# The loop over pairs of token tiles of a Mamba and MLP layer, written out

## The chip, the cores and the metric

The kernel runs on one core of a Trainium2 chip. The metric is the device time of one execution in microseconds. Engines are named as in the profile: PE (TensorE matmul), PEld (its weight loads), DVE (VectorE), ACT (ScalarE), POOL (GpSimd), SP (SyncE, which here only issues transfers). A q behind a name (DVEq) is the engine's queue, in which register and branch instructions run.

## What is computed

The input is x of 4 x 1024 tokens with 256 features. Cut to what matters:

```
x = x + attn(layernorm(x))
x = x + ffn(layernorm(x))
attn(u):  z, x, B, C, dt = split(rmsnorm(u) @ in_proj.T);  dt = softplus(dt @ dt_proj.T + dt_b)
          h = exp(dt * A) * h + (dt * x) * B      # step by step along the tokens
          y = sum over the state of h * C         # 8 groups, 32 states, 32 channels each
          h = u + ((y + x * D) * silu(z)) @ out_proj.T
          h + (silu(n @ gate.T) * (n @ up.T)) @ down.T,  n = rmsnorm(h)
ffn(x):   hidden = silu(x @ W1.T) * (x @ W3.T);  fwht(hidden) @ W2.T
```

## The kernel before, in words

The 4096 tokens are worked through in 8 tiles of 512, two tiles for each of the 4 sequences. An even tile starts a sequence; an odd one goes on with the state that the even one left in `carry`.

For one tile there are 64 units (U). A unit is one scan over 512 tokens for 128 rows of state. The chain of a unit: PE spreads a row of dt into a bank `p_dt` (`spread`, L413; three banks), ACT takes the exponential in it (`decay`, L551), DVE scans (`scan`, L791) with `bt_s`, the driven input. For each pair of units DVE (L776) or POOL (L968) first multiplies `bt_s` with B, and POOL afterwards multiplies `h_s` with C (L988; in even tiles the last column is kept in `carry` before, L985). PE adds up the states of four units in `p_y` (`sum_states`, L424).

The dense work of neighbouring tiles is laid between the units. `body(i, par, pre, units, post)` is one turn of 64 slots u: it holds the units of tile i (`units`), the projections for tile i + 1 (`pre`), and the end of tile i - 1, that is out projection, MLP and second block (`post`). Which dense step stands in which slot comes from the table STEPS, made once by `place_steps`. Every engine has its own `body`, and `bodies` calls it in the same order on each of the five: written out for -1, 0 and 1, then a loop of two passes over the pairs (2, 3) and (4, 5), then written out for 6, 7 and 8. par is i modulo 2 and picks buffers; it is a constant, so a loop body holds two turns.

At a turn's start, on DVE: the last work of the turn before (L868, the low part of dt; L905, the last addition to `res`), the product L776, scans u = 0 to 3, then L798 and L804, which finish y of tile i - 1 and wait for PE's last sum of its states (L424).

All engines meet over semaphores that only count up. So a wait for tile i is a wait for a count such as i * U + u + 1. In a body that is written out i is a Python integer and the count a constant. In the loop i is a register value, and the count is worked out by a register operation on the engine's queue ahead of the wait. `known(i)` tells the two apart; `from_tile(i, least)` is true in the loop, where i is at least 2.

In DVE's scan (L780 to L792) the waits stand in this order: a_dA (the exponential), for even u the driven input (g_bt or v_bt) and, in odd tiles, the carry (g_car), then pe_y. PE's spread waits for the scan that last used the bank.

Of the kernel before, what the change touches and what calls it, by code (L numbers as in the profile page):

```python
# [26 lines left out]
LAST = TILES - 1  # L27
# [87 lines left out]
def build(nc, x, in_w, dt_w, dt_b, a_log, d_par, out_w, gu_w, down_w, n1, n2, w1, w3, w2, ident, pick, ysel, had, out):  # L115
    with ExitStack() as ctx:
# [110 lines left out]
        def bodies(eng, body):  # L227


            body(-1, 1, True, False, False)  # L230
            body(0, 0, True, True, False)
            body(1, 1, True, True, True)
            with eng.Fori(1, LAST // 2) as pair:
                body(pair * 2, 0, True, True, True)
                body(pair * 2 + 1, 1, True, True, True)
            body(LAST - 1, 0, True, True, True)
            body(LAST, 1, False, True, True)
            body(LAST + 1, 0, False, False, True)
# [13 lines left out]
        def _(sp):  # L252
# [66 lines left out]
            def body(i, par, pre, units, post):  # L319
# [11 lines left out]
                for u in range(U):  # L331
# [8 lines left out]
                    if pre:  # L340
# [16 lines left out]
                        if u == 63:  # L357
                            keep_rows(nt, 1 - par, 1)
                            load_b(nt, 1)
                            load_dt(nt, 1)  # L360

            bodies(sp, body)
            sp.wait_ge(l_out, 16 * TILES)


        @block.tensor
        def _(pe):
# [144 lines left out]
            pe.wait_ge(w_in, 2)  # L512
            pe.wait_ge(l_w["c"], 80)
            bodies(pe, body)


        @block.scalar
        def _(act):
# [221 lines left out]

            x_spread(0)
            bodies(act, body)


# [345 lines left out]
```

## Time and profile before

| | us |
|---|---|
| median of 3 runs | 1263.95 (1263.41 to 1265.72) |
| the profiled execution | 1264.71 |
| its span, first to last instruction | 1263.0 |
| PE busy | 1080.1 |
| DVE busy | 1065.1 |
| POOL busy | 958.0 |
| ACT busy | 636.1 |
| mean granted clock of TensorE | 0.936 of full speed |

Busy times are sums over the whole span; the first tiles and the end are less full than the middle. Register, branch and transfer-issuing instructions are not in them. The profile says for each idle stretch of an engine which event ended it; "issue" means that the engine waited for nothing that the profile shows.

### The profile page before, as it was taken

What the parts mean: (1) busy time and instruction counts of PE and PEld (TensorE: products, weight loads), DVE (VectorE), ACT (ScalarE), POOL (GpSimd) and SP (SyncE); (2) the same over time, 40 slices, a digit from 0 to 9 for tenths busy, and PEclk for the clock granted to TensorE, in tenths of its full rate; (3) what the DMA queues carried; (4) which work ended last, traced back from release to release, by engine and by line L of the source; (5) the groups of instructions that cost most, each with busy time, mean ns of one, the idle gap of its engine ahead of it and who ended that gap; (6) DMA issues with size and microseconds to landing.
All of it is one profiled execution on the core that took longest, in us unless ns stands there. A gap on an engine that the chain in (4) does not pass through costs nothing.

```text
span 1263.0 us, 14738 instructions
## 1 busy us (share of the span) xinstructions
PE 1080.1 (86%) x3848; PEld 542.2 (43%) x3848; DVE 1065.1 (84%) x1193; ACT 636.1 (50%) x1142; POOL 958.0 (76%) x580
## 2 busy tenths in 40 slices
PE   2475649999798979899898989899898979898888
PEld 1121214535344444445444444445443544446445
DVE  3288999999998989999899889998999889996222
ACT  3755365545655465545655555545654545442210
POOL 0389998887998788887998888887998789865100
PEclk9676679999998999999899989999999999898889
DMA  5797867574866666684767675684766666650000
GB/s 195 170 250 162 200 152 164 121 179 105 196 134 155 146 156 144 133 187 112 173 136 164 141 165 130 135 187 110 188 135 142 147 154 133 134 117 17 1 0 17
DMA packets 99511, 176.55 MB, mean 140 GB/s; under 512 B 12960, under 2 KB 21600, under 8 KB 98784
## 3 DMA queue, kind: packets, MB, share of 16 engines
q1 hardware_dynamic: 98272, 171.36, 59.7%
q0 software_dynamic: 1152, 4.19, 0.9%
q8 instruction: 34, 0.56, 0.2%
q14 instruction: 53, 0.43, 0.1%
HBM read 150.34 MB, written 8.39 MB: 126 GB/s over the span
## 4 chain that ended last, share of the span: by engine, by line
POOL 29%; issue 25%; PE 16%; ACT 2%; DVE 2%; POOLq 1%; DVEq 0%; ACTq 0%
POOL h_s L988 16%; POOL bt_s L968 7%; PE p_r L458 5%; PE p_r L469 5%; PE p_r L464 2%; PE p_dt L413 2%; PE p_y L424 2%; POOL carry L985 1%; PE p_r L475 1%; POOL sp_l L999 1%; DVE h_s L791 1%; POOL res L1017 1%; POOL sp_w L1003 1%; POOL rs L957 1%; ACT p_dt L551 1%
## 5 line engine op out<-in xcount | busy, mean ns | idle before, releaser
L988 POOL TENSOR_TENSOR h_s<-h_s,c_s 128x1024 f32<-128x1024 f32 x256 | 607.9, 2376 | 104.5 <-DVE h_s L791 94.5
L551 ACT ACTIVATE p_dt<-p_dt,an_s 128x512 f32<-128x512 f32 x512 | 334.5, 658 | 308.1 <-PE p_dt L413 307.7
L413 PE MATMUL p_dt<-kdt,pick_s 128*128 128x512 f32 x512 | 349.5, 692 | 77.9 <-DVE h_s L791 75.5
L791 DVE TENSOR_TENSOR_SCAN h_s<-p_dt,carry,bt_s 128x512 f32<-128x512 f32 x256 | 320.6, 1270 | 14.1 <-ACT p_dt L551 13.6
L791 DVE TENSOR_TENSOR_SCAN h_s<-p_dt,bt_s 128x512 f32<-128x512 f32 x256 | 304.1, 1210 | 31.8 <-ACT p_dt L551 25.4
L469 PE MATMUL p_r<-nT,w_s 128*128 128x512 f32 x512 | 243.8, 604 | 5.4 <-ACT nT L716 5.4
L968 POOL TENSOR_TENSOR bt_s<-bt_s,b_s 128x1024 f32<-128x1024 f32 x96 | 227.2, 2367 | 19.1 <-DMA bt_s<-dx_rows 18.4
L413 PEld LDWEIGHTS p_dt<-kdt,pick_s 128*128 128x128 f32 x512 | 101.3, 201 | 222.9 <-DVE h_s L791 139.4
L776 DVE TENSOR_TENSOR bt_s<-bt_s,p_b 128x1024 f32<-128x1024 f32 x160 | 192.9, 1205 | 2.2 <-DMA bt_s<-dx_rows 1.0
L458 PE MATMUL p_r<-nT,gu_s 128*128 128x512 f32 x352 | 169.9, 603 | 2.3 <-ACT nT L711 2.3
L424 PE MATMUL p_y<-h_s,ysel_s 128*32 128x512 f32 x1024 | 150.5, 663 | 21.5 <-POOL h_s L988 21.5
L469 PEld LDWEIGHTS p_r<-nT,w_s 128*128 128x128 f32 x512 | 95.0, 191 | 122.4 <-issue 114.0
L475 PE MATMUL p_r<-w_s,hd_s 128*128 128x256 f32 x512 | 125.0, 385 | 0.0
L444 PE MATMUL p_r<-uT_s,in_s 128*128 128x512 f32 x192 | 107.2, 666 | 12.5 <-ACT uT_s L653 5.6
L475 PEld LDWEIGHTS p_r<-w_s,hd_s 128*128 128x128 f32 x512 | 96.7, 191 | 28.8 <-issue 14.9
L464 PE MATMUL p_r<-down_s,hd_s 128*128 128x256 f32 (+1 forms) x384 | 100.8, 394 | 0.0
L458 PEld LDWEIGHTS p_r<-nT,gu_s 128*128 128x128 f32 x352 | 64.8, 191 | 79.4 <-issue 73.6
L738 ACT ACTIVATE th_s<-p_r 128x512 f32<-128x512 f32 x64 | 38.2, 597 | 119.7 <-PE p_r L469 119.7
L464 PEld LDWEIGHTS p_r<-down_s,hd_s 128*128 128x128 f32 (+1 forms) x384 | 68.1, 188 | 35.2 <-issue 25.9
L930 DVE SCALAR_TENSOR_TENSOR th_s<-th_s,p_r 128x512 f32<-128x512 f32 x64 | 43.1, 674 | 35.6 <-ACT th_s L738 35.3
L439 PE MATMUL p_r<-ident_s,tok 128*128 128x128 f32 x192 | 31.8, 312 | 44.9 <-ACT tok L568 33.0
L985 POOL TENSOR_TENSOR carry<-h_s,one_s 128x2 f32<-128x2 f32 x128 | 30.1, 236 | 47.2 <-DVE h_s L791 46.3
(92 smaller groups left out, 857.3 us busy)
## 6 DMA issues: line engine op xcount, KB each, us to landing
bt_s<-dx_rows SPq DMA_DIRECT2D x512, 256.0 KB, 5.4
kdt<-st_dt SPq DMA_DIRECT2D x64, 128.0 KB, 3.8
tok<-in_x SPq DMA_DIRECT2D x8, 512.0 KB, 6.9
xr_s<-xb_s SPq DMA_DIRECT2D x64, 64.0 KB, 4.0
dx_rows<-sp_w SPq DMA_DIRECT2D x16, 256.0 KB, 2.0
b_s<-xb_s SPq DMA_DIRECT2D x64, 64.0 KB, 2.0
xo<-in_x SPq DMA_DIRECT2D x8, 512.0 KB, 7.1
out<-res POOLq DMA_DIRECT2D x8, 512.0 KB, 6.3
```

Source lines behind the costliest of these rows:

```text
L413: nc.tensor.matmul(p_dt[DT_BANK[u]][:, :], sel, kdt[:, h, p // 16, :], start=True, stop=True)\
L424: last = nc.tensor.matmul(p_y[32 * j:32 * j + 32, :], ysel_s[:, 28 - 4 * row:60 - 4 * row], h_s[:, u % 8, :], start=(m % 8 == 0), stop=(m ...
L444: ins = nc.tensor.matmul(ps[:, :], in_s[:, j, blk, :], uT_s[:, u_par, j, :], start=(j == 0), stop=(j == 1))
L458: ins = nc.tensor.matmul(ps[:, :], gu_s[:, j, blk, :], nT[:, j, :], start=(j == 0), stop=(j == 1))
L464: ins = nc.tensor.matmul(ps[:, D * (j // 6):D * (j // 6) + D], hd_s[0:n_in, f, P * s:P * s + P], down_s[0:n_in, f, :], start=(f == 0), sto ...
L469: ins = nc.tensor.matmul(ps[:, :], (w1_s if stage == "w1" else w3_s)[:, j, P * k:P * k + P], nT[:, j, :], start=(j == 0), stop=(j == 1))
L475: ins = nc.tensor.matmul(ps[:, D * (j // 8):D * (j // 8) + D], hd_s[:, f, P * s:P * s + P], w2_s[:, f, :], start=(f == 0), stop=(f == HB - 1))
L551: A(p_dt[DT_BANK[u]][:, :], p_dt[DT_BANK[u]][:, :], ACT.Exp, scale=an_s[:, c:c + 1]).then_inc(a_dA, 1)
L776: V.tensor_tensor(bt_s[:, two, :], bt_s[:, two, :], p_b[:, :].unsqueeze(1).broadcast_to([P, 2, T]), ALU.mult).then_inc(v_bt, 1)
L791: V.tensor_tensor_scan(h_s[:, u % 8, :], p_dt[DT_BANK[u]][:, :], bt_s[:, u % 16, :], carry[:, u:u + 1] if par else 0.0, ALU.mult, ALU.add) ...
L968: G.tensor_tensor(bt_s[:, two, :], bt_s[:, two, :], b_s[:, h, :].unsqueeze(1).broadcast_to([P, 2, T]), ALU.mult).then_inc(g_bt, 1)
L988: G.tensor_tensor(h_s[:, two, :], h_s[:, two, :], c_s[:, h, :].unsqueeze(1).broadcast_to([P, 2, T]), ALU.mult)\
```

## The change

The hardware loop becomes a Python loop. Each engine's program now holds the bodies of tiles 2, 3, 4 and 5 one behind the other, with constants as counts.

```
@@ -230,7 +230,7 @@
             body(-1, 1, True, False, False)
             body(0, 0, True, True, False)
             body(1, 1, True, True, True)
-            with eng.Fori(1, LAST // 2) as pair:
+            for pair in range(1, LAST // 2):
                 body(pair * 2, 0, True, True, True)
                 body(pair * 2 + 1, 1, True, True, True)
             body(LAST - 1, 0, True, True, True)
```

LAST is 7, so pair is 1 and 2 in both. What the engines compute and the order in which they do it stay. The register operations (in these listings ISA and REGISTER_ALU) and the branch go.

DVE at the top of the loop, before (L776 is the driven input, L791, listed as SCALAR_TENSOR_TENSOR, the scan, L798 the end of y):

```order
L233 UNCONDITIONAL_BRANCH
L233 ISA
L775 ISA
L776 TENSOR_TENSOR bt_s<-bt_s,p_b 128x1024
L781 ISA
L784 ISA
L790 ISA
L791 SCALAR_TENSOR_TENSOR h_s<-p_dt,bt_s 128x512
L781 REGISTER_ALU
```

The same place in the changed kernel:

```order
L868 TENSOR_TENSOR st_dt<-sp_l,st_dt 128x512
L905 TENSOR_TENSOR res<-p_r,res 128x512
L776 TENSOR_TENSOR bt_s<-bt_s,p_b 128x1024
L791 SCALAR_TENSOR_TENSOR h_s<-p_dt,bt_s 128x512 x2
L776 TENSOR_TENSOR bt_s<-bt_s,p_b 128x1024
L791 SCALAR_TENSOR_TENSOR h_s<-p_dt,bt_s 128x512 x2
L798 SCALAR_TENSOR_TENSOR p_y<-xr_s,par_s,p_y 128x512
```

Nothing is left between the vector instructions.

PE at the top of the loop, before (L413 is the spread, L424 the sum of states, L444 the projections from uT_s, L439 transposes):

```order
L424 MATMUL p_y<-h_s,ysel_s 32x512 x4
L413 MATMUL p_dt<-kdt,pick_s 128x512
L233 UNCONDITIONAL_BRANCH
L233 ISA
L413 MATMUL p_dt<-kdt,pick_s 128x512
L381 REGISTER_ALU
L402 ISA
L442 ISA
L444 MATMUL p_r<-uT_s,in_s 128x512
```

And in the changed kernel:

```order
L424 MATMUL p_y<-h_s,ysel_s 32x512 x4
L413 MATMUL p_dt<-kdt,pick_s 128x512 x2
L444 MATMUL p_r<-uT_s,in_s 128x512 x2
L413 MATMUL p_dt<-kdt,pick_s 128x512
L439 MATMUL p_r<-ident_s,tok 128x128 x8
```

The matmuls follow one another in the same order, without the branch.

## Rows read from the trace of the kernel before

**Rows 1.** The page, busy time by engine (share of the span)

```profile
PE 1080.1 (86%) x3848; PEld 542.2 (43%) x3848; DVE 1065.1 (84%) x1193; ACT 636.1 (50%) x1142; POOL 958.0 (76%) x580
```

**Rows 2.** Windows, tiles 1 to 6: us, busy by engine, granted clock, DMA share, GB/s

```profile
181.14:321.18 140.04, 129.35 (x484) 66.28 (x480) 133.70 (x148) 77.80 (x141) 116.59 (x57) 0.98 0.66 147
321.18:460.87 139.69, 129.59 (x488) 65.78 (x480) 128.54 (x150) 77.74 (x142) 122.02 (x88) 0.98 0.66 150
460.87:601.47 140.60, 128.77 (x484) 65.53 (x480) 134.44 (x150) 77.60 (x142) 117.72 (x58) 0.98 0.66 151
601.47:742.47 141.00, 131.40 (x479) 66.92 (x476) 128.67 (x149) 77.85 (x141) 121.94 (x88) 0.96 0.67 149
742.47:884.68 142.21, 131.81 (x491) 66.31 (x489) 134.42 (x150) 78.42 (x142) 117.66 (x58) 0.97 0.65 149
884.68:1022.98 138.30, 126.94 (x488) 64.97 (x480) 127.11 (x141) 77.51 (x138) 121.87 (x88) 1.00 0.66 148
```

**Rows 3.** Line L233: count, duration ns min/median/max, first and last start

```profile
L233 DVEq FUSED_REGOPS  x2: 63/63/63, 320.6 to 604.1; - x2
...
L233 PEldq FUSED_REGOPS  x2: 50/50/50, 321.3 to 605.6; - x2
...
L233 DVEq COMPARE_BRANCH  x2: 55/59/63, 601.1 to 884.1; - x2
...
L233 PEldq COMPARE_BRANCH  x2: 83/2012/3942, 601.6 to 884.8; - x2
```

**Rows 4.** Timeline of DVE, tile 4: start, us, line, what, [idle before, releaser]

```profile
601.39 1.35 DVE L868 TENSOR_TENSOR st_dt<-sp_l,st_dt 128x512 fp32r<-128x512 f32 x1
...
604.32 1.22 DVE L776 TENSOR_TENSOR bt_s<-bt_s,p_b 128x1024 f32<-128x1024 f32 x1 [0.98 <-issue]
...
613.13 0.76 DVE L798 SCALAR_TENSOR_TENSOR p_y<-xr_s,par_s,p_y 128x512 f32<-128x512 f32 x1 [1.94 <-PE p_y L424]
```

**Rows 5.** Timeline of PE behind the branch

```profile
605.72 0.49 PE L413 MATMUL p_dt<-kdt,pick_s 128*128 128x512 f32 x1 [1.76 <-issue]
```

**Rows 6.** Timeline of DVE, start of tile 2

```profile
321.10 1.34 DVE L868 TENSOR_TENSOR st_dt<-sp_l,st_dt 128x512 fp32r<-128x512 f32 x1
...
330.93 0.76 DVE L798 SCALAR_TENSOR_TENSOR p_y<-xr_s,par_s,p_y 128x512 f32<-128x512 f32 x1 [1.15 <-PE p_y L424]
```

**Rows 7.** Timeline of DVE, start of tile 6

```profile
884.60 1.34 DVE L868 TENSOR_TENSOR st_dt<-sp_l,st_dt 128x512 fp32r<-128x512 f32 x1
...
894.49 0.76 DVE L798 SCALAR_TENSOR_TENSOR p_y<-xr_s,par_s,p_y 128x512 f32<-128x512 f32 x1 [1.21 <-PE p_y L424]
```

**Rows 8.** DMA queues from 596 to 616 us: packets, MB, share

```profile
q14 instruction: 7, 0.06, 1.0%
```

**Rows 9.** Line L781 (the count of the scan's first wait) in DVE's queue

```profile
L781 DVEq ALU_OP  x254: 40/40/52, 321.8 to 880.0; - x127
```

**Rows 10.** Timeline of DVE, scan u=56 of tiles 1 and 3

```profile
303.99 1.28 DVE L791 TENSOR_TENSOR_SCAN h_s<-p_dt,carry,bt_s 128x512 f32<-128x512 f32 x1 [1.34 <-ACT p_dt L551]
584.28 1.28 DVE L791 TENSOR_TENSOR_SCAN h_s<-p_dt,carry,bt_s 128x512 f32<-128x512 f32 x1 [1.61 <-ACT p_dt L551]
```

**Rows 11.** Timeline of DVE, scan u=56 of tiles 2, 4 and 6

```profile
443.75 2.34 DVE L791 TENSOR_TENSOR_SCAN h_s<-p_dt,bt_s 128x512 f32<-128x512 f32 x2 [1.70 <-ACT p_dt L551]
725.35 2.34 DVE L791 TENSOR_TENSOR_SCAN h_s<-p_dt,bt_s 128x512 f32<-128x512 f32 x2 [1.70 <-ACT p_dt L551]
1006.46 2.39 DVE L791 TENSOR_TENSOR_SCAN h_s<-p_dt,bt_s 128x512 f32<-128x512 f32 x2 [1.53 <-ACT p_dt L551]
```

**Rows 12.** Timeline of PE, the same matmuls in tiles 3 and 5

```profile
468.96 1.13 PE L444 MATMUL p_r<-uT_s,in_s 128*128 128x512 f32 x2 [1.08 <-ACT uT_s L653]
750.53 2.05 PE L444 MATMUL p_r<-uT_s,in_s 128*128 128x512 f32 x2 [1.08 <-ACT uT_s L653]
```

**Rows 13.** Windows of 3.4 us in tiles 5 and 4, columns as in rows 2

```profile
750.60:754.00 3.40, 3.40 (x11) 0.95 (x11) 1.39 (x2) 1.03 (x2) 3.40 (x2) 0.50 1.03 238
607.20:610.60 3.40, 3.40 (x11) 2.06 (x9) 3.40 (x4) 2.32 (x5) 2.89 (x3) 0.50 0.83 239
```

More of the change, by code:

```diff
@@ L232, in bodies @@
             body(1, 1, True, True, True)
-            with eng.Fori(1, LAST // 2) as pair:
+            for pair in range(1, LAST // 2):
                 body(pair * 2, 0, True, True, True)
```

## The prediction

> **What bounds the kernel now.** I read the page's busy times first: PE 86% and DVE 84% of the span [rows 1]. Neither is full, and the two wait for each other: PE spreads a channel's time steps, ACT takes the exponential, DVE scans, and PE may refill the bank only after the scan. So a stall on any of the three moves the whole line unless a longer wait stands behind it.
>
> Then I cut the trace into tiles. A tile here runs from the end of the 64th scan (L791) of the tile before to the end of its own 64th; what the tile before has left over (L868, L905) falls into it. Tiles 1 and 6 run from code that is written out already, tiles 2 to 5 from the loop; so the profile of before holds both forms side by side. The table [rows 2] gives 140.04, 139.69, 140.60, 141.00, 142.21 and 138.30 us for tiles 1 to 6. Odd tiles are to be compared with tile 1, even ones with tile 6, because odd and even bodies differ (carry). Two corrections are needed. Tile 6 is lighter than the others at its end: it prepares no statistics for a later tile. So I compare even tiles only as far as their scan u=56. And tile 1 lacks the last addition of a tile before it (L905) and one output transfer; its total of 140.04 may therefore flatter written-out code by a few tenths, which the bounds take up.
>
> **Part 1: the jump back.** There is one, since two passes run: from the end of tile 3's body to the start of tile 4's. Read the branch line itself [rows 3]: DVE's branch stands at 601.1 us and takes about 0.06, but the register operation at the top of the body comes at 604.1; on PE 601.6 and 605.6, with a branch record of 3.94 us. So three engines that depend on each other issue nothing for 3 to 4 us. What was already queued covers part: DVE still runs L868 and L905 and is idle for 0.98 us "issue" before L776 [rows 4]; PE is idle 1.76 us "issue" before its next spread [rows 5]. The price is read where the line is whole again, at L798, the first DVE work that waits for all of PE, POOL and DVE. From L868 to L798 it is 613.13 - 601.39 = 11.74 us in tile 4 [rows 4], against 330.93 - 321.10 = 9.83 in tile 2, which the loop enters from above with no jump [rows 6], and 894.49 - 884.60 = 9.89 in written-out tile 6 [rows 7]. So **the jump costs 1.9 us**, and comparing tile 4 with tile 6 at u=56 (below) shows that nothing later gives it back. Entering the loop costs nothing that shows (9.83 against 9.89), nor does leaving it.
>
> A rule speaks against so high a price. The Trainium skill, Advanced Engine Details and Errata, section Control Flow Timing, puts a compare-and-branch at some 108 ns; by that alone the jump would be worth 0.1 us and the whole edit, with part 2, 1.6 us. The trace disagrees as to what follows the branch: the branch record of DVE is short, the silence behind it is 3.0 us. The skill's Runtime: NRT & Kernel Launch, section Instruction fetch mechanics, says that a taken branch outside the fetched pages must fetch its target first; the trace agrees: 7 instruction packets on one queue in the 20 us around the jump [rows 8].
>
> **Part 2: counters in registers.** In the loop each wait on a count that depends on the tile needs a register operation before it, 306 on DVE for the two tiles of a pass in the listing of its instructions; those of L781 take 40 ns each [rows 9]. Most cost nothing: they run in the queue while DVE, ACT or PE executes earlier work. That cover is gone when the engine has run dry and the scan has several waits one behind the other: the first is met late, and then the registers for the next are computed. The scan u=56 shows it. In tile 1 it starts 303.99, after 1.34 us idle; in tile 3 after 1.61, with the same releaser, ACT's L551 [rows 10]: 0.27 us more. In even tiles it is 1.70 in the loop against 1.53 in tile 6 [rows 11]: 0.17. I take the sum from whole stretches. Odd: tile 3 less tile 1, 140.60 - 140.04 = 0.56. Even: from L868 to scan u=56 tile 4 takes 725.35 - 601.39 = 123.96 and tile 6 takes 1006.46 - 884.60 = 121.86 [rows 4, 7, 11]; of the 2.10 the jump is 1.9, so 0.2 is left. Two odd and two even tiles: 2 x 0.56 + 2 x 0.2 = **1.5 us**. Bounds: not below 0 (nothing is added), hardly above 2.2 (0.56 in all four). SP and POOL lose register operations too; SP's transfers wait for scans, POOL's for h_s, so I cost both at 0.
>
> **Part 3: TensorE's clock, which I leave as it is.** Tile 5 is 1.61 us longer than tile 3 with the same code. PE's two matmuls of L444 plus the next spread take 2.05 us at 750.53 where tile 3's take 1.13 [rows 12], in a stretch where the granted clock is 0.50, that is 1.2 GHz instead of 2.4 [rows 13]; the later work of the tile keeps that distance. Tile 2 also lost: its L868 to u=56 is 443.75 - 321.10 = 122.65, 0.79 above tile 6, of which 0.2 is part 2 and the remaining 0.6 I put to a step of the clock in its middle. Steps near a tile's start or middle come in straight tiles as well; PE has waited shortly before. They depend on small shifts in time, so I expect other ones after the change, of about the same sum. The bounds: all of 1.61 + 0.6 = 2.2 us goes as well, or two further steps of 1.6 us come.
>
> **Sum.** 1.9 + 1.5 = 3.4 us of the profiled execution's 1264.71 (span 1263.0), which is 0.76 above the median of the runs, 1263.95. I take the difference from the median: 1263.95 - 3.4 = 1260.5 us. Nothing is late next: where the jump stood, L798 waits for PE's L424 as it does in tile 2, 1.15 us idle [rows 6].
>
> **Rivals.**
> - *The clock steps go too.* The 3 to 4 us silence on PE lies beside them, and a straight tile 6 has none. Then 3.4 + 2.2 = 5.6 us, 1258.3. Against it: tile 5 is far from the jump. Chance 0.20.
> - *The jump itself is cheap*, and the 1.9 us come from the lowered clock that tile 4 has just behind it at 607 us [rows 13] and keeps without the jump. Then part 2 alone remains: 1.5 us, 1262.4. For it: such a step costs 1.6 us in tile 5. Against it: DVE's 0.98 and PE's 1.76 us of "issue" lie before that step. Chance 0.10. By the Trainium skill's Control Flow Timing (Advanced Engine Details and Errata) the time would be the same within 0.1 us.
> - *One clock step more than now, or part 2 near 0* because tile 1 flattered: 3.4 - 1.6 = 1.8 or 1.9 us, 1262.1. For it: tiles 4 and 5 both have a step near their start. Against it: tiles 2, 3 and 6 have none. Chance 0.23.
> - *Slower:* written-out code shifts the tile starts so that PE's wait before L444 meets a lowered clock in nearly every tile. Price 1.6 us each; the saved 3.4 are gone with the third additional step, and from the fourth (6.4 - 3.4 = 3.0 us slower, 1266.9) it can be told. Tiles 2, 3 and 6 without such a step speak against it. Chance 0.05.
> - *That the edit does nothing* can be excluded: the order of instructions shows no branch and no register operation left on DVE, PE, ACT and SP.
>
> **How the numbers follow.** About 0.2% (2.5 us) is what a measurement of this kernel can tell from no change: faster begins at 1261.4. My forecast, 3.4 us with steps of the clock that sum up to the same, holds 0.42; together with the first rival faster has 0.62. The two rivals of small gains are within 0.2%: 0.10 + 0.23 = 0.33. Slower 0.05. The range goes from 1258.0 (all steps gone, part 2 at its upper bound in part) to 1263.5 (two more steps and 0.4 us less from part 2, 1263.95 - 3.4 + 3.2 - 0.2).
>
> **What would show it.** Right: from L868 to L798 tile 4 takes 9.8 to 9.9 us; DVE and PE have no "issue" gap there; the idle time before scan u=56 is 1.34 in tiles 3 and 5 and 1.53 in tiles 2 and 4; tile 3 takes 140.0. Wrong: a gap of "issue" in a written-out tile, at a place where instructions are fetched; tile 4 at 141 without a jump; or the 3.4 us appear and go again into L444 at a clock of 0.50.

## The result and the profile after

The changed kernel takes 1260.59 us (median of 13 runs, 1258.91 to 1262.12), the kernel before, timed beside it, 1264.37 (13 runs, 1263.14 to 1266.74). The ratio is 0.9968, interval 0.9960 to 0.9977: **faster by 4.0 us (2.9 to 5.1)**, 0.3% of the time. The prediction was 1260.5 in a range of 1258.0 to 1263.5, with 3.4 us to be won. Number and sign hold; two of the three terms behind the number were mis-sized, as the experiments show.

The profiled execution of the changed kernel took 1260.81 us, its span is 1259.0 after 1263.0. First its busy times, against [rows 1]: nearly the same work on the engines, 4 us less span.

```profile
PE 1075.6 (85%) x3848; PEld 540.7 (43%) x3848; DVE 1064.8 (85%) x1193; ACT 636.4 (51%) x1142; POOL 957.5 (76%) x580
```

Now the tiles, the table that answers to [rows 2] (us, busy by engine, granted clock, DMA share, GB/s; tiles 1 to 6, each from the end of one tile's last scan to the end of the next one's):

```profile
180.63:320.63 140.00, 129.31 (x484) 66.22 (x480) 133.68 (x148) 77.79 (x141) 116.52 (x57) 0.98 0.65 147
320.63:459.59 138.96, 126.90 (x488) 64.88 (x480) 128.75 (x150) 77.66 (x142) 121.97 (x88) 1.00 0.67 151
459.59:600.42 140.83, 129.16 (x488) 65.66 (x480) 134.90 (x149) 78.26 (x142) 117.75 (x58) 0.98 0.65 151
600.42:739.90 139.48, 129.38 (x488) 65.81 (x480) 128.74 (x149) 77.73 (x142) 121.76 (x88) 0.98 0.65 150
739.90:880.20 140.30, 128.56 (x488) 65.63 (x480) 134.57 (x150) 78.05 (x142) 117.69 (x58) 0.99 0.65 151
880.20:1019.09 138.89, 129.49 (x488) 65.92 (x480) 127.12 (x140) 77.58 (x138) 121.78 (x88) 0.98 0.65 147
```

Less before: tile 1 -0.04, tile 2 -0.73, tile 3 +0.23, tile 4 -1.52, tile 5 -1.91, tile 6 +0.59. The stretch ahead of tile 1 gives -0.51 and what follows tile 6 -0.1. So the gain lies in tiles 2, 4 and 5, while tile 3 and the untouched tile 6 are longer. That tile 6 moves by 0.6 us with the same instructions says that single executions carry a second effect of that size: TensorE's clock.

The start of tile 4, where the jump was, on DVE (start, us, line, what, [idle before, releaser]), to be read against [rows 4]:

```profile
600.34 1.34 DVE L868 TENSOR_TENSOR st_dt<-sp_l,st_dt 128x512 fp32r<-128x512 f32 x1
601.60 0.68 DVE L905 TENSOR_TENSOR res<-p_r,res 128x512 f32<-128x512 f32 x1
602.20 1.20 DVE L776 TENSOR_TENSOR bt_s<-bt_s,p_b 128x1024 f32<-128x1024 f32 x1
...
610.21 0.76 DVE L798 SCALAR_TENSOR_TENSOR p_y<-xr_s,par_s,p_y 128x512 f32<-128x512 f32 x1 [1.20 <-PE p_y L424]
```

L776 follows without a gap, and from L868 to L798 it is 9.87 us, not 11.74. PE keeps one "issue" pause of 0.79 us there, ahead of L444. It needs no fetch to explain it: tile 2 of the kernel before, entered without a jump, stood still at the same place for 0.83 us (put down there to DVE's L905), and the prediction overlooked that when it said that PE would have no such gap.

Scan u=56 of tiles 2, 3, 4 and 5, which answers to [rows 10, 11]:

```profile
442.41 2.39 DVE L791 TENSOR_TENSOR_SCAN h_s<-p_dt,bt_s 128x512 f32<-128x512 f32 x2 [1.52 <-ACT p_dt L551]
...
583.23 2.46 DVE L791 TENSOR_TENSOR_SCAN h_s<-p_dt,carry,bt_s 128x512 f32<-128x512 f32 x2 [1.34 <-ACT p_dt L551]
...
722.73 2.39 DVE L791 TENSOR_TENSOR_SCAN h_s<-p_dt,bt_s 128x512 f32<-128x512 f32 x2 [1.52 <-ACT p_dt L551]
...
863.01 2.46 DVE L791 TENSOR_TENSOR_SCAN h_s<-p_dt,carry,bt_s 128x512 f32<-128x512 f32 x2 [1.34 <-ACT p_dt L551]
```

1.70 has become 1.52 and 1.61 has become 1.34, within 0.01 us the values of the tiles that were written out before. And the clock: a window in the middle of tile 4 and one in tile 3.

```profile
671.50:678.30 6.80, 5.72 (x13) 2.00 (x14) 6.75 (x7) 4.09 (x10) 6.64 (x6) 0.50 0.48 118
531.50:538.30 6.80, 4.81 (x12) 1.67 (x13) 6.76 (x11) 4.05 (x9) 6.56 (x6) 0.50 0.53 128
```

Both stand at 0.50, 1.2 GHz, for 6.8 us. Before, tiles 3 and 4 had 3.4 us at that level there. So part of what tiles 3 and 4 won went again into PE at half clock. Tile 3 was to take 140.0 us and took 140.83.

### The profile page after: what moved, and what is told of

It is laid out like the page before. It is cut to its first block, busy times and chain, and to the rows that moved or that the text cites. A ratio compares the mean times of both kernels' runs of the same rounds, so it can differ in the third digit from the quotient of the medians.

```text
span 1259.0 us, 13157 instructions
## 1 busy us (share of the span) xinstructions
PE 1075.6 (85%) x3848; PEld 540.7 (43%) x3848; DVE 1064.8 (85%) x1193; ACT 636.4 (51%) x1142; POOL 957.5 (76%) x580
## 4 chain that ended last, share of the span: by engine, by line
PE 50%; POOL 13%; issue 13%; ACT 11%; DVE 8%; DMA 2%; SPq 2%; POOLq 0%; DVEq 0%; ACTq 0%
PE p_r L469 16%; PE p_r L458 12%; POOL h_s L988 6%; PE p_y L424 6%; PE p_dt L413 5%; PE p_r L444 4%; DVE h_s L791 3%; ACT p_dt L551 2%; PE p_r L464 2%; POOL bt_s L968 2%; PE p_r L453 2%; DMA bt_s<-dx_rows 2%; ACT tok L568 2%; DVE sp_l L854 1%; POOL sp_l L999 1%
## 5 line engine op out<-in xcount | busy, mean ns | idle before, releaser
L413 PE MATMUL p_dt<-kdt,pick_s 128*128 128x512 f32 x512 | 348.3, 691 | 77.0 <-DVE h_s L791 76.6
L791 DVE TENSOR_TENSOR_SCAN h_s<-p_dt,carry,bt_s 128x512 f32<-128x512 f32 x256 | 320.9, 1271 | 12.9 <-ACT p_dt L551 12.5
L791 DVE TENSOR_TENSOR_SCAN h_s<-p_dt,bt_s 128x512 f32<-128x512 f32 x256 | 304.4, 1211 | 31.6 <-ACT p_dt L551 24.9
L413 PEld LDWEIGHTS p_dt<-kdt,pick_s 128*128 128x128 f32 x512 | 101.0, 200 | 219.4 <-DVE h_s L791 140.2
L776 DVE TENSOR_TENSOR bt_s<-bt_s,p_b 128x1024 f32<-128x1024 f32 x160 | 193.0, 1206 | 1.0 <-DMA bt_s<-dx_rows 0.7
L424 PE MATMUL p_y<-h_s,ysel_s 128*32 128x512 f32 x1024 | 149.2, 657 | 19.6 <-POOL h_s L988 19.6
L444 PE MATMUL p_r<-uT_s,in_s 128*128 128x512 f32 x192 | 106.4, 661 | 16.0 <-issue 7.1
L439 PE MATMUL p_r<-ident_s,tok 128*128 128x128 f32 x192 | 30.9, 306 | 45.1 <-ACT tok L568 33.4
```

The costliest lines, as they stand in the source:

```text
L413: nc.tensor.matmul(p_dt[DT_BANK[u]][:, :], sel, kdt[:, h, p // 16, :], start=True, stop=True)\
L424: last = nc.tensor.matmul(p_y[32 * j:32 * j + 32, :], ysel_s[:, 28 - 4 * row:60 - 4 * row], h_s[:, u % 8, :], start=(m % 8 == 0), stop=(m ...
L444: ins = nc.tensor.matmul(ps[:, :], in_s[:, j, blk, :], uT_s[:, u_par, j, :], start=(j == 0), stop=(j == 1))
L776: V.tensor_tensor(bt_s[:, two, :], bt_s[:, two, :], p_b[:, :].unsqueeze(1).broadcast_to([P, 2, T]), ALU.mult).then_inc(v_bt, 1)
L791: V.tensor_tensor_scan(h_s[:, u % 8, :], p_dt[DT_BANK[u]][:, :], bt_s[:, u % 16, :], carry[:, u:u + 1] if par else 0.0, ALU.mult, ALU.add) ...
```

## The experiments

Two questions were left: is it the branch, or the fetch behind it, and on which engine; and what part has the clock that steps down just behind the jump in tile 4 [rows 13], a rival in the prediction. In the experiments' listings line numbers are shifted by up to 5; names tell what is meant. "L868 to L798" is st_dt to p_y in tile 4.

**A near jump.**

```
 for pair in range(1, LAST // 2):
     ...
+    if pair == 1:
+        with eng.Fori(0, 2) as again:
+            eng.wait_ge(w_zero, 2)
```

> The changed kernel with one taken branch per engine put back between tiles 3 and 4, but to a target one instruction away (a loop of two passes over a wait that is already met). Theory: the 1.9 us of the jump were the fetch of the instructions at a far target, so a near jump costs next to nothing: from L868 to L798 tile 4 takes 9.8 to 10.1 us, as in tiles 2 and 6 (9.83, 9.89), and the time stays at 1260 to 1261. Rival: it is the branch itself, or the halt of the queue at it, that costs; then L868 to L798 takes about 11.7 and the time is near 1262.5.

Measured: 1261.10 us, ratio to before 0.9978 (0.9964 to 0.9993). DVE in tile 4:

```profile
599.78 1.35 DVE L871 TENSOR_TENSOR st_dt<-sp_l,st_dt 128x512 fp32r<-128x512 f32 x1
609.67 0.76 DVE L801 SCALAR_TENSOR_TENSOR p_y<-xr_s,par_s,p_y 128x512 f32<-128x512 f32 x1 [1.21 <-PE p_y L427]
```

That is 9.89 us, the same as with no branch. The branch lines themselves (count, ns min/median/max, first and last start):

```profile
L237 DVEq COMPARE_BRANCH  x2: 50/56/63, 599.4 to 599.7; - x2
...
L237 PEldq COMPARE_BRANCH  x2: 76/152/228, 600.1 to 600.5; - x2
```

DVE's two branches lie 0.3 us apart with a wait and a register operation between; in the loop 3.0 us passed behind the branch [rows 3]. A branch as such costs nothing that shows here. The Trainium skill puts a compare-and-branch at about 108 ns (Advanced Engine Details and Errata, Control Flow Timing); the records of this near jump are of that size, 50 and 63 ns on DVE and 76 and 228 ns on PE.

What the far jump adds can be counted in the instruction packets of the whole span (packets, MB, share). The kernel before, then the near jump:

```profile
q8 instruction: 34, 0.56, 0.2%
q14 instruction: 53, 0.43, 0.1%
```

```profile
q8 instruction: 31, 0.51, 0.2%
q14 instruction: 39, 0.32, 0.1%
```

The changed kernel has 31 and 39 as well, so the near jump fetches nothing more, while the loop fetches 17 packets more although its program is shorter. With the loop on PE alone it is 34 and 39, on DVE alone 31 and 45, on ACT alone 31 and 43: each engine that jumps back fetches for itself. In the 17 us around the near jump there is no instruction packet at all; in the 20 us around the jump of before there are the seven of [rows 8] on one queue and two on q8, PE's, which the prediction left out.

**The loop on one engine alone.** This asks which engine's jump and which engine's registers count. Three kernels, in which `bodies` gets the loop for one engine and is written out for the other four:

```
+def bodies(eng, body, looped=False):
...
+            if looped:
+                with eng.Fori(1, LAST // 2) as pair:
...
+            else:
+                for pair in range(1, LAST // 2):
```

> The loop kept on PE alone, with its registers; DVE, ACT, POOL and SP written out. Theory: PE's silence of 4 us at the jump sets L798, so L868 to L798 in tile 4 takes 11.5 to 11.8 us as before, and the scan u=56 of tiles 3 and 5 starts after 1.34 us idle, since the registers that delayed it were DVE's. Rival: DVE's jump sets it; then 9.8 to 10.3 us here. Time 1262 to 1263 by the theory, near 1260.5 by the rival.

> The loop kept on DVE alone. Theory: DVE's own gap of about 1 us before L776 returns in tile 4, but L798 waits for PE anyway (1.15 us idle in tile 2), so L868 to L798 takes 9.8 to 10.2 us; the idle time before scan u=56 is again 1.61 in tiles 3 and 5 and 1.70 in 2 and 4, and about 0.2 to 0.3 us a tile are lost by it. Time about 1 us over the changed kernel. Rival: the jump's price is DVE's, L868 to L798 takes 11 us or more.

> The loop kept on ACT alone. Theory: ACT comes 0.6 us late to L568 in tile 4, PE's transposes wait for it, so L868 to L798 takes 10.2 to 10.6 us; registers of ACT cost nothing else, u=56 idles 1.34. Time at most 0.7 us over the changed kernel. Rival: ACT, which stands between PE and DVE for each unit, carries the jump's full price: 11.5 us or more.

Each ratio is to runs of the kernel before on the same chip (for these three and the near jump 31 runs, 1264.65 us).

| loop on | median us | ratio to before | L868 to L798, tile 4 | idle before u=56, tiles 3 / 4 |
|---|---|---|---|---|
| all (before) | 1264.37 | 1 | 11.74 | 1.61 / 1.70 |
| PE | 1263.34 | 0.9991 (0.9974 to 1.0008) | 11.67 | 1.34 / 1.52 |
| DVE | 1261.15 | 0.9981 (0.9966 to 0.9997) | 9.88 | 1.60 / 1.69 |
| ACT | 1260.24 | 0.9979 (0.9963 to 0.9995) | 10.25 | 1.34 / 1.53 |
| none (changed) | 1260.59 | 0.9968 (0.9960 to 0.9977) | 9.87 | 1.34 / 1.52 |

With the loop on PE, DVE has no gap of its own, yet L798 is as late as before (first two rows; the third is PE behind its branch, the fourth the window of its clock):

```profile
598.17 1.34 DVE L873 TENSOR_TENSOR st_dt<-sp_l,st_dt 128x512 fp32r<-128x512 f32 x1
609.84 0.76 DVE L803 SCALAR_TENSOR_TENSOR p_y<-xr_s,par_s,p_y 128x512 f32<-128x512 f32 x1 [1.73 <-PE p_y L429]
```

```profile
602.05 0.79 PE L418 MATMUL p_dt<-kdt,pick_s 128*128 128x512 f32 x1 [2.86 <-issue]
```

```profile
601.50:604.90 3.40, 2.85 (x4) 1.58 (x5) 3.40 (x4) 2.43 (x5) 3.37 (x3) 0.50 0.68 156
```

With the loop on DVE alone the gap is there, 0.81 us, and is absorbed by the time that L798 waits for PE: its idle time falls to 0.29.

```profile
602.00 1.35 DVE L873 TENSOR_TENSOR st_dt<-sp_l,st_dt 128x512 fp32r<-128x512 f32 x1
604.76 1.22 DVE L781 TENSOR_TENSOR bt_s<-bt_s,p_b 128x1024 f32<-128x1024 f32 x1 [0.81 <-issue]
611.88 0.76 DVE L803 SCALAR_TENSOR_TENSOR p_y<-xr_s,par_s,p_y 128x512 f32<-128x512 f32 x1 [0.29 <-PE p_y L429]
```

So the jump's price is PE's; ACT's alone would be 0.3 to 0.4 us (10.25 against 9.98 in tile 2 of the same trace and 9.87 in the changed kernel), and prices of the engines do not add up, since their silences lie side by side. The registers' price is DVE's: its loop alone brings back 1.60 and 1.69. The medians of the three do not tell so fine a difference.

**The registers, with the loop kept.** The trace of before shows the delay itself. Ahead of scan u=56 in tile 3, which starts at 584.28, stand three register operations (columns as in [rows 9]):

```profile
L786 DVEq ALU_OP  x1: 40/40/40, 584.0 to 584.0; - x1
L788 DVEq ALU_OP  x1: 40/40/40, 584.1 to 584.1; - x1
L790 DVEq ALU_OP  x1: 40/40/40, 584.2 to 584.2; - x1
```

In tile 2, where the scan starts at 443.75 and there is no wait for the carry, there are two:

```profile
L786 DVEq ALU_OP  x1: 40/40/40, 443.6 to 443.6; - x1
L790 DVEq ALU_OP  x1: 40/40/40, 443.7 to 443.7; - x1
```

They follow one another about 0.09 us apart: three make the 0.27 us and two the 0.17. As a test, the wait for a_dA was put last in the scan:

```
-                dve.wait_ge(a_dA, n + 1)
                 if u % 2 == 0:
...
                     dve.wait_ge(pe_y, i * (U // 4) + u // 4 - 1)
+                dve.wait_ge(a_dA, n + 1)
```

> The kernel before with its loop, but in the scan the wait for the exponential (a_dA, the one that is met last) stands behind the other waits instead of ahead of them. Theory of the registers: what delayed the scan u=56 by 0.27 and 0.17 us were the register operations for the other waits, which ran only after a_dA was met; now they are done by then. So u=56 idles 1.34 us in tiles 3 and 5 and 1.53 in 2 and 4 although all registers are still there, and u=56 comes at 121.8 us in a tile 2 without a clock step (written out 121.78). The jump stays: L868 to L798 in tile 4 11.7. Time 1262.5 to 1264, about 1 us under before. Rival: the registers cost by their number, wherever they stand; then 1.61 and 1.70 as before.

Scan u=56 in tiles 2 and 3, with every register operation still in place:

```profile
444.47 2.40 DVE L791 TENSOR_TENSOR_SCAN h_s<-p_dt,bt_s 128x512 f32<-128x512 f32 x2 [1.52 <-ACT p_dt L551]
```

```profile
584.78 2.46 DVE L791 TENSOR_TENSOR_SCAN h_s<-p_dt,carry,bt_s 128x512 f32<-128x512 f32 x2 [1.34 <-ACT p_dt L551]
```

The 0.27 and 0.17 us are gone, and tiles 3 and 5 take 140.33 us instead of 140.60: at these scans a register operation cost time only behind a wait that was met late. But the time did not fall, 1264.12, ratio 1.0001 (0.9986 to 1.0016), a miss of the expected microsecond. In the profiled execution tile 4 shows a reason: from L868 to L798 it took 13.14 us.

```profile
601.89 1.35 DVE L868 TENSOR_TENSOR st_dt<-sp_l,st_dt 128x512 fp32r<-128x512 f32 x1
...
615.03 0.76 DVE L798 SCALAR_TENSOR_TENSOR p_y<-xr_s,par_s,p_y 128x512 f32<-128x512 f32 x1 [1.79 <-PE p_y L424]
```

```profile
604.60:611.40 6.80, 4.89 (x9) 2.54 (x10) 5.71 (x5) 3.76 (x8) 5.92 (x7) 0.51 0.75 189
```

The jump is the same; the clock is at half for 6.8 us from 2.8 us after L868. That broke my fixed price of 1.9 us and led to the last group below.

**The same order in the written-out kernel.** Same edit on the changed kernel.

> The same new order of waits in the changed kernel. Theory: nothing is worked out between its waits, so nothing is to be won: u=56 idles 1.34 and 1.52, and comes at 121.8 (even) and 123.1 us (odd) in tiles without a clock step; time as the changed kernel, within its spread. Rival: waits as such, behind one another, cost some tens of ns each where a_dA is late; then the tiles are 0.1 to 0.3 us shorter.

Measured 1262.92, ratio to before 0.9989 (0.9979 to 0.9999); u=56 idles 1.42 in tile 3 and 1.59 in tile 4, 0.07 us more than in the changed kernel. Nothing is won, as the theory had it. The intervals of this ratio and of the changed kernel's just miss each other, so the order may even lose a little. Tiles 3 and 5 took 140.48 us, 0.2 more than in the changed kernel; that does not add up to 2 us, and I leave the rest open.

**PE kept busy in its pauses.** Extra matmuls, whose results are overwritten, were put into two pauses of PE, in the hope that the clock would stay up:

```
+                    if stage == "dtr" and j == 0:
+                        fill(ps, 1)
...
+                    if u == 34 and units and pre:
+                        q = PLAN.index(("c0", 0, 2, .86))
+                        bank_free(q, i, on)
+                        fill(ring[q % RING], 2)
```

> The changed kernel with PE kept busy in two of its pauses: one matmul of 128x512 f32 whose result is overwritten before dtr waits for uT_s at a tile's start (pause of 1.2 us), and two before spread 36 waits for its scan in the middle (pause of 2.5 us). Theory of the clock steps: they follow PE's pauses; then the stretches at 0.5 at 3 to 11 us and at 68 to 78 us into tiles 1 to 6 are gone, u=56 comes at 121.8 and 123.1 in all tiles, spans scatter less, and the time is 1 to 2 us under the changed kernel, 1258.5 to 1260. Rival: the steps come at other places or from something else; then as many remain and the added 3 us of PE work a tile cost up to 0.5 us a tile: 1260.5 to 1263.

Measured 1265.73, ratio 1.0012 (1.0000 to 1.0024), 5 us over the changed kernel. The rival holds as to the clock: a stretch at half clock remained in or at the edge of every tile from 1 to 6. Those in the middle went from tiles 3 and 5, came 6 to 9 us later in tiles 1, 4 and 6, and one was added (in tile 2 for 6.8 us from 79 us into it, where the changed kernel has none). The price was higher than the rival had it, 1260.5 to 1263: tile 2 took 141.62 us and tile 1 141.93. The added matmuls themselves ran at full clock in tiles 1 to 6, 0.59 us each. This version is no gain.

**More traces of the same kernels, and PE held without a branch.** The kernel before twice, the changed one and the loop on PE once more, and a kernel in which PE is held at tile starts by a wait alone:

```
+                    if u == 0 and 2 <= i <= 6:
+                        pe.wait_ge(v_sc, i * U + 1)
                     if (units if u + 2 < U else pre):
                         spread(i + (u + 2) // U, (u + 2) % U)
```

> The kernel before once more, unchanged, for a second trace. Theory: the price of the jump is fixed, L868 to L798 in tile 4 takes 11.7 us again, and u=56 idles 1.61 and 1.70; but clock steps lie elsewhere, so tile 5 need not be 1.6 us longer than tile 3 and tile 2 need not lose 0.6. Rival: these two losses belong to the loop and come again at the same tiles.

> The kernel before, a third trace. Theory: L868 to L798 in tile 4 is 10.7 us if no clock step lies 2 to 9 us into the tile and 11.7 or more if one does. Rival, as the prediction had it: always 11.7.

> The changed kernel, a second trace: L868 to L798 9.9 in tiles 2, 4 and 6 and 10.7 in 3 and 5, with no clock step 2 to 9 us into tiles 2 to 6 or at most one; tiles 2 to 5 together 558.5 to 560 us.

> The loop on PE alone, a second trace: as in the kernel before, 10.7 us without and 11.7 or more with a clock step 2 to 9 us into tile 4; u=56 idles 1.34 and 1.52.

> The changed kernel with PE held, without any branch, at the start of tiles 2 to 6: before spread u=2 it also waits for the scan u=0, which lets it go about 4.2 us after the tile's start, near the 4.6 us of the jump. Theory now: the jump costs 0.85 us by the pause itself and 1 to 2.4 us more where TensorE's clock steps down behind PE's pause; the branch has no part in it. Then L868 to L798 takes 10.5 to 10.9 us in even tiles without a step and 11.6 to 13.2 in those with one, and steps come 2 to 9 us into most of the five tiles. Time 1264 to 1270. Rival: the pause alone brings no step; what brought it was the fetch or chance. Then no tile is over 10.9 (even) or 11.6 (odd), time near 1264.

The second trace of before was to show 11.7 us again. It has the jump and no lowered clock behind it, and takes 10.74 (DVE, then the window):

```profile
599.47 1.33 DVE L868 TENSOR_TENSOR st_dt<-sp_l,st_dt 128x512 fp32r<-128x512 f32 x1
...
602.41 1.22 DVE L776 TENSOR_TENSOR bt_s<-bt_s,p_b 128x1024 f32<-128x1024 f32 x1 [1.00 <-issue]
...
610.21 0.76 DVE L798 SCALAR_TENSOR_TENSOR p_y<-xr_s,par_s,p_y 128x512 f32<-128x512 f32 x1 [0.97 <-PE p_y L424]
```

```profile
602.00:609.00 7.00, 4.73 (x18) 2.48 (x17) 6.59 (x6) 5.34 (x10) 6.08 (x6) 1.00 0.70 196
```

All traces with a jump on PE, tile 4, with PE's idle time at the jump:

| trace | PE idle | L868 to L798 | time at 0.50 behind the jump |
|---|---|---|---|
| before, second | 1.54 | 10.74 | none |
| before, third | 1.54 | 10.67 | none |
| loop on PE, second | 3.03 | 10.60 | none |
| loop on PE, first | 2.86 | 11.67 | 3.4 us |
| before, first | 1.76 | 11.74 | 3.4 us |
| late wait in the loop | 3.60 | 13.14 | 6.8 us |
| written out, both traces | | 9.87 | none |

In the three traces of before PE goes into the jump at half clock; this is the second one:

```profile
598.40:601.80 3.40, 3.40 (x13) 0.86 (x11) 3.01 (x3) 1.02 (x2) 3.40 (x2) 0.50 0.55 160
```

So its matmuls last longer there and PE's idle time is shorter. That stretch costs at most 0.1 us: with it tile 2 takes 9.88 and 9.91 us from L868 to L798 in the second and third trace, without it 9.83 in the first.

So **the jump costs 0.7 to 0.9 us by its pause, 1.8 to 1.9 with 3.4 us of low clock behind it and 3.3 with 6.8 us**. The clock has its part in the price, but not as the prediction's rival had it, as something that stays without the jump: in the two traces of the changed kernel no tile from 2 to 6 has low clock in the first 9 us after its start. The second of these took 558.2 us for tiles 2 to 5, just under the expected 558.5 to 560.

The held kernel shows whether a pause brings it. It took 1275.19 us, ratio 1.0092 (1.0058 to 1.0126). PE in tile 4, and the clock in tiles 2 to 6:

```profile
610.15 0.80 PE L413 MATMUL p_dt<-kdt,pick_s 128*128 128x512 f32 x1 [3.24 <-DVE h_s L793]
610.74 3.62 PE L444 MATMUL p_r<-uT_s,in_s 128*128 128x512 f32 x4
```

```profile
325.20:328.60 3.40, 2.57 (x4) 1.44 (x5) 3.40 (x4) 2.34 (x5) 3.37 (x3) 0.55 0.78 202
468.60:472.00 3.40, 3.40 (x7) 1.51 (x6) 2.80 (x3) 1.42 (x4) 3.37 (x3) 0.54 0.88 218
608.50:615.30 6.80, 5.15 (x10) 2.79 (x11) 4.95 (x5) 3.52 (x7) 6.62 (x7) 0.52 0.88 205
751.90:758.70 6.80, 5.03 (x9) 2.67 (x10) 5.20 (x5) 3.44 (x7) 6.62 (x7) 0.52 0.84 190
895.30:902.10 6.80, 5.28 (x11) 2.92 (x12) 4.82 (x5) 3.65 (x7) 6.62 (x7) 0.52 0.85 198
```

Five of five tiles step down, with no branch in the program; L444's four matmuls take 3.62 us instead of 1.96. L868 to L798 is 12.11, 12.93 and 12.93 us in tiles 2, 4 and 6 (9.9 without the hold). The theory's mechanism holds; its time, 1264 to 1270, was too low, since I priced too few double steps and nothing for their sum: 2.1 to 3.1 us in each of five tiles at L798 alone make 13.

The held pauses are 3.23 to 3.98 us of idle PE. So a pause of that length is shown to bring the step. For the shorter ones it is not: behind the jump 3.03 us had none and 1.76 had one. This is the second trace of the loop on PE, where the clock is at full from the middle of tile 3 to the middle of tile 4:

```profile
604.83 0.50 PE L418 MATMUL p_dt<-kdt,pick_s 128*128 128x512 f32 x1 [3.03 <-issue]
```

Finally, what the prediction took for parts of the loop in single tiles. Tile 5 took 142.21 us in the first trace of before [rows 2], 140.60 in the second: its 1.61 us was a clock step alone. In the third it took 142.08, with 6.8 us at half clock in its middle instead of 3.4. Tile 2 took 122.57 us up to u=56 in the first trace, with 6.8 us at half clock in its middle, and 122.02 and 122.09 in the other two, without it. Written out it takes 121.78 and 121.75. So 0.5 of its 0.8 us was clock.

## Why the prediction was right, and where it was not

**Part 1, the jump: right in mechanism, wrong as one number.** "The jump costs 1.9 us" came from one trace, at [rows 4, 6], and that trace held a stretch of low clock behind the jump [rows 13]. The step that failed is the reading that 11.74 - 9.83 is the jump's alone. It is 0.8 us of pause on PE, plus 1.0 in that execution from the clock, which steps down behind the pause in some executions and not in others. That the pause brings it on is shown for longer pauses, in the held kernel, and argued for this one of 1.76 us. The mean is 1.2 us over the three traces of before and 1.6 over all six with a jump on PE. The argument that the two idle gaps "lie before that step" did not look at the stretch just ahead: PE was at half clock from 600.4 to 603.8 us as well. The Trainium skill (Runtime: NRT & Kernel Launch, Instruction fetch mechanics) says that a taken branch to a target outside the fetched pages has to fetch it before the engine goes on. The near jump (9.89 us, no packet more) and the loop (10.67 us and more, 17 packets more) agree.

**Part 2, the registers: 1.2 us, not 1.5.** The mechanism stands: the register operations lie in the gap, the loop on DVE alone brings the delays back, the late wait takes them away. Mis-sized was the term for odd tiles, 0.56 each, from tile 3 less tile 1. Tile 1 flattered: it lacks L905 and the output transfer, and the written-out tile 3 reaches u=4 0.29 us later than tile 1. Compared with the same 3.4 us at half clock in the middle and no more, an odd tile takes 140.60 in the loop (three traces) and 140.30 written out (140.31, 140.29): 0.3 us. Even tiles lose 0.3 up to u=56 (122.02 and 122.09 against 121.75 and 121.78), where the prediction had 0.2. The loop on DVE alone gives the same without a jump on PE: 140.57 and 140.56 for tiles 3 and 5, and 122.08 in tile 4, which has no low clock at all. Together 4 x 0.3 = 1.2.

**Part 3, the clock: "about the same sum" was not so for this pair.** Tile 5's 1.6 us and tile 2's 0.5 went; 0.5 to 0.6 us each came in tiles 3, 4 and 6. That is some 0.4 us in favour of the changed kernel in this pair of traces. The second trace of the changed kernel has them in tiles 4 and 6 and not in tile 3, which took 140.31.

**The sum.** For the two first traces: jump with its clock 1.9, registers 1.2, clock elsewhere 0.4, the stretch ahead of tile 1 0.5: 4.0, as between the spans. The last two are chance: tile 1 begins at 181.14, 179.80 and 179.47 us in the three traces of before. For the medians only 1.2 + 1.2 to 1.6 + 1.2, 2.4 to 2.8 us of 4.0 (2.9 to 5.1), is shown, just below the interval. The measurement leaves room for that: the near-jump kernel, which is the changed one with a branch that costs nothing, has in its own runs the ratio 0.9978, 2.8 us less than before (0.9 to 4.6). What is left may also be more stretches of low clock in the loop kernel: in the same series its mean granted clock over 31 runs is 0.933, and 0.935 to 0.937 in the 30 runs of the three kernels whose PE is written out; the ten with the loop on PE have 0.935 too, so the clock alone does not mark the loop. This is argued and not shown, as only three traces of before exist. So the predicted 3.4 lies near the measured value in part by luck: the oversized 1.9 and 1.5 made up for what was not priced. And the upper end of the range is not the sum that it names: two more steps and 0.4 us less from part 2 give 1263.95 - 3.4 + 3.2 + 0.4 = 1264.15, not 1263.5.

Of the rivals, "the jump itself is cheap" was half right (0.8 us) and wrong in that the low clock would stay. Of "the clock steps go too" the two that it named went, but others came. Steps near the start of nearly every tile, the slower case, did not come in written-out code; in the held kernel, where they did, pause and step together cost 2.1 to 3.1 us a tile and not 1.6.

## What to carry to other kernels

The price of this loop's back edge was what PE lost while its first instructions were fetched; the other engines' silences of about the same length hid behind it. So look first at the engine that the others wait for at the top of the loop. Do not take such a price from one trace if the clock stepped in it: look for the same place in tiles without a step, or in a second execution. And where counts sit in registers, put the wait that is met last at the end, so that what has to be worked out is done before; here it won nothing that could be timed, but the delay of the scan was gone. With constants as counts the same order won nothing and idled 0.07 us more.

## What was not expected of the hardware

- A pause of 3.2 to 4.0 us on PE, made by a wait alone, was followed by 3.4 or 6.8 us at half clock in 5 of 5 tiles. Behind the jump, where PE was idle for 1.5 to 3.6 us, this came in 3 of 6 traces, and it made a 0.8 us stall one of 1.8 to 3.3.
- A taken branch to a near target, on all five engines, left L868 to L798 within 0.02 us (9.89 against 9.87), while a far one silenced DVE for 2.9 to 3.5 us and PE for 3.5 to 4.3.
- Filling PE's pauses with extra matmuls did not keep the clock up; the low stretches came later and the kernel lost 5 us.
